# Attention on one core: paired row-maximum reductions, four banks for maxima and two for scores

## What is computed

```python
scores = jnp.einsum('bqhd,bkhd->bhqk', q, k)
scores = scores + jnp.einsum('bqr,bkr->bqk', q_rope, k_rope)[:, None]
scores = scores / scale
scores = jnp.where(causal[None, None], -jnp.inf, scores)
w = jax.nn.softmax(scores, axis=-1)
attn = jnp.einsum('bhqk,bkhd->bqhd', w, v).reshape(Bb, Tt, D_MODEL)
return attn @ W_o
```

## Time and profile before

| | |
|---|---|
| median of 3 runs | 3594.57 us (3592.02 to 3594.73) |
| the profiled execution's own time | 3594.03 us |
| its span, first to last instruction | 3592.3 us |
| attention, from the first to the last score | about 460 to 2806 us of the span |
| granted TensorE clock, mean | 0.991 |

### The profile page before, as it was taken

The page is one execution under the profiler, slowest core; times in us unless marked ns, Lnnn a source line. Parts: engine busy times, 40 slices in busy tenths (PEclk is TensorE's granted clock), DMA queues, the critical chain, the costliest instruction groups (busy, mean ns, idle before and its releaser), DMA issues. The chain is left out here.

```text
span 3592.3 us, 54217 instructions
## 1 busy us (share of the span) xinstructions
PE 3497.8 (97%) x19552; PEld 2403.9 (67%) x19552; DVE 2542.4 (71%) x5361; ACT 1790.6 (50%) x3423; POOL 2668.6 (74%) x1194
## 2 busy tenths in 40 slices
PE   8999989999999999999999999999999699999999
PEld 4777756666666666666666666666665488888887
DVE  6777777777777777777777777777775466666665
ACT  2333345555555555555555555555555344434443
POOL 2333268889889898898988988989889556666665
PEclk9999999999999999999999999999999799999999
DMA  5789754463453634625346354363461112222220
GB/s 204 285 281 315 276 126 97 98 139 83 115 125 88 138 83 100 148 71 133 88 108 139 80 118 113 90 144 80 105 150 48 62 59 71 71 71 71 71 71 36
DMA packets 232757, 426.59 MB, mean 119 GB/s; under 512 B 25380, under 2 KB 26916, under 8 KB 232488
## 3 DMA queue, kind: packets, MB, share of 16 engines
q1 hardware_dynamic: 232424, 423.10, 43.8%
q10 hardware_dynamic: 64, 0.02, 0.0%
HBM read 300.86 MB, written 121.65 MB: 118 GB/s over the span
## 5 line engine op out<-in xcount | busy, mean ns | idle before, releaser
L1057 ACT ACTIVATE att_probs<-att_ps_s 128x512 f32<-128x512 f32 (+3 forms) x2560 | 1300.4, 535 | 936.9 <-PE att_ps_s L1218 847.2
L1157 POOL TENSOR_TENSOR att_sum_g<-att_sum_g,att_probs 128x2048 f32<-128x2048 f32 (+3 forms) x400 | 1624.4, 4061 | 73.1 <-ACT att_probs L1057 34.4
L1093 DVE TENSOR_REDUCE att_piece_max<-att_ps_m 128x1 f32<-128x512 f32 x1520 | 945.2, 681 | 128.4 <-PE att_ps_m L1201 126.9
L1217 PE MATMUL att_ps_s<-att_q_a,att_k_a 128*128 128x512 f32 (+3 forms) x2560 | 950.9, 373 | 12.3 <-DMA att_k_b<-s_kr_hi 8.2
L1218 PE MATMUL att_ps_s<-att_q_b,att_k_b 65*128 65x512 f32 (+3 forms) x2560 | 933.9, 367 | 0.0
L1096 DVE CUSTOM_DVE_ANT_0 att_ps_m<-att_ps_m,mask_qk 128x128 f32<-128x128 f32 x1008 | 477.5, 508 | 269.9 <-PE att_ps_m L1201 256.9
L1201 PE MATMUL att_ps_m<-att_k_a,att_q_a 128*128 128x512 f32 (+3 forms) x1808 | 650.3, 383 | 6.6 <-DVE att_piece_max L1096 3.5
L1217 PEld LDWEIGHTS att_ps_s<-att_q_a,att_k_a 128*128 128x128 f32 x2560 | 485.7, 190 | 124.8 <-ACT att_probs L1057 42.5
L1224 PE MATMUL att_ps_o<-att_probs,att_v 128*32 128x512 f32 (+3 forms) x5120 | 547.2, 536 | 4.4 <-POOL att_probs L1137 4.4
L1218 PEld LDWEIGHTS att_ps_s<-att_q_b,att_k_b 65*128 65x128 f32 x2560 | 484.2, 189 | 65.5
L1201 PEld LDWEIGHTS att_ps_m<-att_k_a,att_q_a 128*128 128x128 f32 x1808 | 340.0, 190 | 226.8 <-issue 76.2
(11 more groups left out here) (190 smaller groups left out, 4938.0 us busy)
## 6 DMA issues: line engine op xcount, KB each, us to landing
att_q_a<-s_q_hi SPq DMA_DIRECT2D x128, 256.0 KB, 6.0
att_q_a<-s_qr_hi SPq DMA_DIRECT2D x128, 256.0 KB, 6.7
prj_x_sb<-in_x_dram SPq DMA_DIRECT2D x16, 1024.0 KB, 5.8
s_q_hi<-prj_q_hi SPq DMA_DIRECT2D x16, 1024.0 KB, 4.2
s_q_lo<-prj_q_lo SPq DMA_DIRECT2D x16, 1024.0 KB, 5.4
s_k_hi<-prj_k_hi SPq DMA_DIRECT2D x16, 1024.0 KB, 4.6
s_k_lo<-prj_k_lo SPq DMA_DIRECT2D x16, 1024.0 KB, 7.0
s_v<-prj_v_sb SPq DMA_DIRECT2D x16, 1024.0 KB, 9.0
```

Source lines behind the costliest of these rows:

```text
L1057: act.activation(probs[t % RING][:, hh, c0:CH], ps_s[(GH * t + hh) % SBANKS][:, c0:CH], ACT.Exp, scale=SCALE).then_inc(probs_ready, 1)
L1093: dve.tensor_reduce(top, ps_m[:, bank, :], AX_X, ALU.max).then_inc(piece_taken, 1)
L1157: pool.tensor_tensor(sum_g[:, :, c0:CH], sum_g[:, :, c0:CH], new, ALU.add).then_inc(sum_added, 1)
L1217: mm(out[:, c0:CH], k_a[:, hh, i * P:(i + 1) * P], q_a[j][:, hh, c0:CH], start=True, stop=False)
```

## The change

A full piece no longer has a reduction of its own: two pieces that follow each other (`r` even and odd) lie in two neighbouring banks, and one TENSOR_REDUCE reads both (128 x 1024 in, 128 x 2 out), after waiting for both. Both banks are released together, when it ends. Diagonal pieces keep their single reductions. `ps_m` gets four banks, `ps_s` keeps two. The bank of an item is written down in `BANK` (a turn takes two places, so that pairs stay on an even bank), and what a bank waits for in `BEFORE`. Pieces are dealt to steps, and within a step to its parts, by even counts (`even_cut`, `deal`), so that the halves of a pair stand together on both engines. The planner's two constants go from 2.8 and 19 to 2.6 and 20.

```diff
--- before.py
+++ after.py
@@ -665,8 +665,8 @@
 NSTEP = sum(STEPS)
 RING = 5
 QB_RING = 3
-SBANKS = 3
-MBANKS = 3
+SBANKS = 2
+MBANKS = 4
 
 
 
@@ -730,7 +730,12 @@
     return own / CH + GH * any(FIRST[j] == (2 * m) % NSTEP for j in range(TCH))
 
 
-PIECE, CLOSING = 2.8, 19
+PIECE, CLOSING = 2.6, 20
+
+
+def even_cut(items, n, parts):
+
+    return len(items) if n == parts else 2 * (len(items) // 2 * n // parts)
 
 
 def deal(items, pairs):
@@ -744,9 +749,9 @@
     out, seen = {}, 0.0
     for m in pairs:
         for half in (0, 1):
-            done = round(seen)
+            done = 2 * round(seen / 2)
             seen += share(high, m % (NSTEP // 2)) / 2
-            out[2 * m + half] = items[done:round(seen)]
+            out[2 * m + half] = items[done:2 * round(seen / 2)]
     assert sum(map(len, out.values())) == len(items)
     return out
 
@@ -891,6 +896,12 @@
         PLAN = maximum_plan()
         ORDER = AHEAD + [it for t in sorted(PLAN) for it in PLAN[t]]
         PLACE = {it: n for n, it in enumerate(ORDER)}
+        BANK, BEFORE, slot, holder = {}, {}, 0, {}
+        for it in ORDER[len(AHEAD):]:
+            BANK[it] = slot % MBANKS
+            BEFORE[it] = PLACE[holder.get(slot % MBANKS, AHEAD[-1])] + 1
+            holder[slot % MBANKS] = it
+            slot += 2 if it[2] == "turn" else 1
         LAST = [it for it in ORDER if it[1:] == max_pieces(it[1])[-1]]
 
         def from_next(item):
@@ -1081,7 +1092,14 @@
             def maxima(items):
 
                 for item in items:
-                    j, seq, bank = item[1], PLACE[item], PLACE[item] % MBANKS
+                    j, seq, bank = item[1], PLACE[item], BANK[item]
+                    if item[2] != "turn" and item[4] < j:
+                        _, _, hh, r, kc = item
+                        if r % 2 == 0:
+                            dve.wait_ge(piece_ready, seq + 2)
+                            dve.tensor_reduce(piece_max[:, j, hh * TB + r:hh * TB + r + 2, kc], ps_m[:, bank:bank + 2, :],
+                                              AX_X, ALU.max).then_inc(piece_taken, 2)
+                        continue
                     dve.wait_ge(piece_ready, seq + 1)
                     if item[2] == "turn":
                         dve.tensor_scalar(neg_max[:, j, :], ps_m[0:GH * TB, bank, 0:P], -1.0, None,
@@ -1089,12 +1107,9 @@
                         continue
                     _, _, hh, r, kc = item
                     top = piece_max[:, j, hh * TB + r, kc:kc + 1]
-                    if kc < j:
-                        dve.tensor_reduce(top, ps_m[:, bank, :], AX_X, ALU.max).then_inc(piece_taken, 1)
-                    else:
-                        width = (r + 1) * P
-                        dve.tensor_tensor_reduce(ps_m[:, bank, 0:width], ps_m[:, bank, 0:width], keep["mask_qk"][:, CH - width:CH],
-                                                 1.0, MASKED, ALU.add, ALU.max, top).then_inc(piece_taken, 1)
+                    width = (r + 1) * P
+                    dve.tensor_tensor_reduce(ps_m[:, bank, 0:width], ps_m[:, bank, 0:width], keep["mask_qk"][:, CH - width:CH],
+                                             1.0, MASKED, ALU.add, ALU.max, top).then_inc(piece_taken, 1)
                     if item in LAST:
                         dve.wait_ge(piece_taken, seq + 1)
                         dve.tensor_reduce(row_max[:, j, :], piece_max[:, j, :, 0:j + 1], AX_X, ALU.max).then_inc(max_ready, 1)
@@ -1117,7 +1132,7 @@
             for t, extra in extras.items():
                 items = PLAN.get(t, [])
                 for n in range(len(extra) + 1):
-                    maxima(items[len(items) * n // (len(extra) + 1):len(items) * (n + 1) // (len(extra) + 1)])
+                    maxima(items[even_cut(items, n, len(extra) + 1):even_cut(items, n + 1, len(extra) + 1)])
                     if n < len(extra):
                         extra[n]()
 
@@ -1179,11 +1194,9 @@
 
             def maximum(item):
 
-                place = PLACE[item]
-                bank = place % MBANKS
+                bank = BANK[item]
                 u, j = item[:2]
-                if place >= MBANKS:
-                    pe.wait_ge(piece_taken, place - MBANKS + 1)
+                pe.wait_ge(piece_taken, BEFORE[item])
                 if item[2] == "turn":
                     pe.wait_ge(max_ready, LAST.index((u, *max_pieces(j)[-1])) + 1)
                     pe.transpose(ps_m[0:GH * TB, bank, 0:P], row_max[:, j, :], keep["ident_f"][:]).then_inc(piece_ready, 1)
@@ -1274,7 +1287,7 @@
                 items = PLAN.get(t, [])
                 for n, part in enumerate(parts):
                     part()
-                    for it in items[len(items) * n // len(parts):len(items) * (n + 1) // len(parts)]:
+                    for it in items[even_cut(items, n, len(parts)):even_cut(items, n + 1, len(parts))]:
                         maximum(it)
 
 
```

## The result

The changed kernel takes 3794.7 us (median, 3792.9 to 3795.1) against 3593.4 for the kernel before: 1.0559 times as long, 95% interval 1.0545 to 1.0572, or 201 us slower. The forecast was 3740, in a range of 3670 to 3820.

What follows compares the result with a forecast made beforehand. PE's own queue, through its waits for banks, was taken to bound the kernel. Against 3594 us, score waits +176, VectorE -40 and +25, and POOL -15 gave +146, so 3740 us, in a range of 3670 to 3820.

Steps and rivals of the forecast that it cites:

- Bound: In attention, PE's own queue sets the pace; only its work or its next instruction's waits for a bank change the time.
- Round trip of a score bank: Full-width scores: a bank comes round in 1.42 us, against 0.94 us of PE work for two scores.
- Main term, +176 us: Rows of scores on two banks: every second score (third, fifth, seventh) waits for ACT's exponential; 189 - 13 = +176 us.
- POOL, -15 us: PE's waits for POOL's sums, 24 + 23 us, shrink as PE slips; -15 us, between 0 and -47.
- VectorE's busy time, 120 us saved: Paired reductions: 1.20 us a pair instead of 1.36 saves DVE 120 us busy time, by itself worth nothing.
- VectorE, -40 us saved: PE's waits for DVE before pieces: at most 82 us to save, at least nothing; taken as -40 us.
- VectorE, +25 us added: Pairs release banks after 2.02 us against 1.88 due, at 163 pair-score-pair-score places, plus longer rows; +25 us, between 0 and 60.
- Dealing and constants, 0 beyond the rows: Planner's constants and even dealing keep pieces and matmuls, only lengthen rows without a piece, already counted; nothing more.
- The rule against the change: Skill's advice to break up instructions of an unsaturated, bubble-causing engine: DVE saving nothing, sum 40 us higher.
- The faster one: Rival: VectorE's waits matter and two score banks suffice, if a bank is released within 0.94 us; 3537 us, chance 0.04.
- the larger one: Rival: tight places tip over (+45), pairs cost 60, nothing is given back; +241 us, 3835 us, chance 0.12.
- The tight places: Some 600 places with 1.41 us of work against 1.42; a trip 0.15 us longer would cost half of them, +45 us.

Runs made afterwards that it cites:

- e1: The kernel before with two score banks instead of three, nothing else changed; 3709.0 us, ratio 1.0326.
- e3: The kernel before, three score and three maxima banks, single reductions, with the change's even dealing and constants 2.6 and 20; 3647.9 us, ratio 1.0155.
- e2: The kernel before with two score banks and four for maxima, single reductions, dealing as before; 3694.1 us, ratio 1.0283.
- e4: The changed kernel with each full piece reduced by its own instruction, releasing its bank at once; 3752.1 us, ratio 1.0448.

## Why the prediction was right, and where it was short

- **Bound.** PE's queue, through waits for banks: right. Work on every engine is the same or less, and the time rose.
- **Round trip of a score bank.** 1.42 us worked out, 1.42 to 1.43 measured in the row of seven. The alternation of starts was there as described, a wait at the third and the fifth score and none between.
- **Main term, +176 us.** Right in mechanism, a little small: the score line of the table grew by 189 us. The two parts of the difference have opposite signs. The third, fifth and seventh scores of a row, which I had priced at 104 + 30 + 40 = 174 us, cost 161 in the trace (99 at full width, 24 at 384 columns, 39 at 256 and behind it), and the 61 narrow places with two pieces between 6 instead of 15. The second, fourth and sixth, which I had called free, cost 37 us. (What fourth scores cost before is 16 us in the trace, where I had taken off 13.) The loader waited for ACT 1030 times, not 300 to 500, but 640 of these waits are under 0.3 us and mostly hidden. e1 priced the same mechanism apart, 116 us against an expected 120 to 150. Its counterpart, that three banks cost nothing even in rows of seven, is shown by e3.
- **POOL, -15 us.** Right: the loss from a score to the closing of denominators fell from 17 to 4 us, and that from values to a closing from 20 to 11.
- **VectorE's busy time, 120 us saved.** Wrong: it fell by 46 us, 60 ns a pair. I had compared the lengths of records, 1.36 us for two against 1.20. But a record is longer than the engine's pace: queued single reductions last 681 ns and start 600 ns apart, queued pairs last 1221 ns and start 1135 ns apart. Nothing of the sum hung on it, since I had given the busy time no worth.
- **VectorE, -40 us saved.** Failed, and this is one of the two steps that made the forecast short. I took half of the bound of the waits as saved. The fourth bank saves 15 us (e2 against e1), and the paired instruction saves nothing that PE sees.
- **VectorE, +25 us added.** Mis-sized, the second step: the pair costs 43 us (changed against e4). The 163 places with pair, score, pair, score were rightly priced: 162 pieces behind a score wait for DVE and lose 27 us there, against 2 in e4. I had not priced the turn, which stands directly behind a pair and loses 10 us more, nor the way from a piece to a piece, which loses 7 more. With both terms right, +28 net stands in place of -15: 43 of the 55 us that the forecast lacked. The rest is near the 13 us of the main term.
- **Dealing and constants, 0 beyond the rows.** With two score banks right in kind: e4 against e2 is 58 us, and e4's score line is 51 us above e2's. That the same dealing costs 55 us with three banks too, by another way (pieces in twos on single banks), was not foreseen.
- **The loss in three steps.** Banks 101 us (e2), dealing and constants on top 58 (e4), paired instruction on top 43. Each kernel adds one part to the one before it, so the sum is the whole by construction; another order of the parts could divide it otherwise.
- **The rule against the change** in the Trainium skill ("Perfetto Trace Analysis", optimizing Scalar/DVE operations: break up the instructions of an engine that isn't saturated but causes bubbles) was the better guide than my middle value. DVE was busy 73% of attention, the pair saved nothing in PE's waits, and e4, which breaks the pairs up again, is 43 us faster. The sum by that rule would have been 3780. The same section's fixed cost, 125 ns of busy time for an operation on PSUM, is not what the trace shows: a merge saved 60 ns of busy time, and 2 x 681 - 1221 = 141 ns of record.
- **Rivals.** The faster one needed a trip under 0.94 us and found 1.42. Of the larger one, the pairs' price came near (43 of 60). It says that nothing is given back, but its own sum keeps the -40; 15 of them came, and POOL's share was given back too. The tight places, some 600 with 1.41 us of work, did not tip as a whole. The result lies between this rival and the forecast.

## What to carry to other kernels

Count the banks of a handover by its round trip (producer's streaming, start of the reader, its whole duration, release and load), not by the reader's rate: two banks carry it only where the producer has that much other work between two uses. Joining two instructions of an engine that has idle time saves busy time that nobody may be waiting for, and delays the start until the last input is there; here that cost 43 us. When banks are traded, price both sides in the order of instructions, including what must be placed together for the trade; here that lengthened the very rows that the lost bank had covered.

## What was unexpected

- Exponentials of 512 columns last 0.60 us but follow each other 0.49 us apart when queued, so the length of a record overstates what ACT needs for each. Even so ACT was idle 0.34 us in every 1.43 in the row of seven: each engine waited for the other.
- A pair of banks was reduced in 1221 ns, 141 ns less than two single reductions by their records, but only some 65 ns less by the distance of starts in a queue. DVE was then more often idle before them (289 us against 127), so its saving turned into waiting.
- The changed kernel is 5 us quicker behind its last score: PE no longer waits 4.40 us for the masked triangle there, and its next value matmuls run at the full clock. How much of the 5 us is the wait and how much the clock, no run separates.
